# Three y buffers instead of five, and other places for the mixed tiles, in a gated attention and expert block

## The reference

```python
x = x + tanh(g_xattn) * xattn(ctx_512, layernorm(x), Wq, Wk, gamma_raw)     # stage 1
h = layernorm(x)                                                           # 2048 tokens of 512
shared = silu(h @ shared_gate_w) * (h @ shared_up_w) @ shared_down_w
top_val, top_idx = top_k(h @ router_w, 2)
probs = zeros.at[token, top_idx].set(sigmoid(top_val))                      # 2 of 8 are not zero
gate, up = split(einsum('etd,edf->etf', probs.T[:, :, None] * h[None], gate_up_w))
out = x + tanh(g_ffn) * (shared + einsum('eti,eid->etd', silu(gate) * up, down_w).sum(axis=0))
```

## Time and profile before

| | us |
|---|---|
| three runs | 394.82, 396.11, 396.09 |
| median | 396.09 |
| the profiled execution | 394.82 |
| its span, first to last instruction | 393.1 |
| TensorE busy | 360.6 |
| VectorE, ACT, POOL busy | 230.7, 211.9, 144.2 |
| mean granted clock of TensorE | 0.973 |

### The profile page before, as it was taken

One profiled execution on the slowest core, in us unless ns is written; L12 is line 12 of the kernel. 1 busy time (PEld: TensorE's weight loads), 2 busy tenths in 40 slices (PEclk: granted clock), 3 DMA queues, 4 the chain that ended last, 5 costly groups with the idle time before them and its releaser, 6 DMA issues.

```text
span 393.1 us, 6569 instructions
## 1 busy us (share of the span) xinstructions
PE 360.6 (92%) x2024; PEld 202.1 (51%) x2026; DVE 230.7 (59%) x820; ACT 211.9 (54%) x412; POOL 144.2 (37%) x123
## 2 busy tenths in 40 slices
PE   8958789989999999999999999999999989999930
PEld 4513478557845589457875444344344434334610
DVE  1899999899999789960846372451451533601200
ACT  2695888476653686435230576566457466363210
POOL 2200121030533342222214364764745654654331
PEclk9987999999999999999999999999999999999975
DMA  7999980276667633449241845746565656576354
GB/s 218 383 387 380 389 286 6 27 206 174 191 112 170 199 61 40 69 113 207 36 53 29 134 72 95 118 77 111 86 115 87 98 107 115 79 119 109 56 75 53
DMA packets 30649, 53.48 MB, mean 136 GB/s; under 512 B 4758, under 2 KB 8086, under 8 KB 30614
## 3 DMA queue, kind: packets, MB, share of 16 engines
q0 software_dynamic: 11216, 24.52, 38.4%
q1 hardware_dynamic: 19110, 28.40, 20.7%
q10 hardware_dynamic: 288, 0.13, 0.1%
HBM read 28.60 MB, written 24.45 MB: 135 GB/s over the span
## 4 chain that ended last, share of the span: by engine, by line
PE 54%; DMA 20%; DVE 10%; issue 7%; ACT 5%; POOL 2%; POOLq 1%; DVEq 0%; ACTq 0%
PE gate_up L1328 14%; PE down L1374 12%; PE gate_up L1339 11%; DMA out_dram<-x,tmp 8%; DMA out_dram<-tmp,idx 5%; DMA out_dram<-y_sb,idx 4%; DMA out_dram<-y_sb,tmp 4%; PE gate_up L1335 4%; PE turned_x L1308 2%; DVE ge_words L1761 2%; ACT junk L731 1%; PE down L1365 1%; PE front L1204 1%; ACT x L768 1%; DVE top L1802 1%
## 5 line engine op out<-in xcount | busy, mean ns | idle before, releaser
L1339 PE MATMUL gate_up<-w_gu,xT 128*128 x192 | 86.2, 593 | 0.0
L1328 PE MATMUL gate_up<-xT,w_shgu 128*128 128x128 f32 x544 | 63.8, 276 | 1.1 <-ACT xT L779 1.1
L1328 PEld LDWEIGHTS gate_up<-xT,w_shgu 128*128 128x128 f32 x544 | 62.2, 192 | 3.6 <-issue 2.3
L565 POOL DMA_INDIRECT xg<-x_rows,idx x34 | 40.4, 1189 | 43.6 <-DMA x_rows<-payl 13.5
L1339 PEld LDWEIGHTS gate_up<-w_gu,xT 128*128 128x128 f32 x192 | 34.8, 190 | 35.9 <-issue 35.9
L2096 DVE SCALAR_TENSOR_TENSOR h<-gate_up,p_t,silu 128x256 f32<-128x256 f32 x33 | 15.9, 483 | 57.8 <-ACT silu L802 48.5
L1374 PE MATMUL down<-w_dn,hT 128*128 x100 | 47.0, 596 | 0.0
L2067 DVE COPY sim<-w_gu 128x2048 f32 x36 | 42.4, 1229 | 1.4 <-issue 0.7
L591 POOL DMA_INDIRECT out_dram<-y_sb,idx x14 | 24.2, 1728 | 44.5 <-ACT y_sb L835 16.3
L731 ACT ACTIVATE junk<-sim,probe 128x512 int8<-128x512 f32 x44 | 31.2, 712 | 14.2 <-DVE probe L1752 7.3
L835 ACT ACTIVATE y_sb<-down,gates 128x512 f32<-128x512 f32 x35 | 23.9, 687 | 27.1 <-PE down L1374 18.1
(11 more groups left out here) (239 smaller groups left out, 545.1 us busy)
## 6 DMA issues: line engine op xcount, KB each, us to landing
w_gu<-in_L_ffn_gate_up_w_dram SPq DMA_DIRECT2D x8, 1024.0 KB, 12.5
xs<-in_x_dram SPq DMA_DIRECT2D x4, 1024.0 KB, 6.9
w_dn<-in_L_ffn_down_w_dram SPq DMA_DIRECT2D x8, 512.0 KB, 10.8
out_dram<-xs SPq DMA_DIRECT2D x4, 1024.0 KB, 6.8
x_rows<-x SPq DMA_DIRECT2D x4, 1024.0 KB, 5.2
out_dram<-y_sb POOLq DMA_DIRECT2D x16, 256.0 KB, 4.3
w_gu<-in_ctx_dram SPq DMA_DIRECT2D x4, 256.0 KB, 5.2
xg<-x_rows,idx POOLq DMA_INDIRECT x34, 4.2
```

The source lines that it names most:

```text
L565: G.indirect_dma_start(out=xg[:, t % XG, :], out_offset=None, in_=x2_rows[0:2 * N, :] if t < EARLY else x2_rows[:, :], in_offset=bass.Indi ...
L1328: mm = TE.matmul(g_b[j % 2][:, f * P:(f + 1) * P], w_shgu[:, c, f * P:(f + 1) * P], xT[:, x_slot(j), c], start=(c == 0), stop=(c == DC - 1))
L1339: mm = TE.matmul(g_b[j % 2][:, :], xT[:, x_slot(j), c], w_gu[:, bass.ds(experts[n] * (DC * F2) + c * F2, F2)], start=(c == 0), stop=(c == ...
```

## The change

Three things. `MIXED` goes from (9, 12, 14, 17, 19, 22, 24, 27, 29) to (9, 11, 13, 15, 18, 21, 24, 27, 30). The calls of `stage_up`, `stage_down` and `scatter_doubles` move with the tiles; all `stage_up` copies of a mixed tile now stand together, where some stood two and two. And the y buffers from job 26 on are three in turn (0, 1, 2) instead of five.

```diff
-    MIXED = (9, 12, 14, 17, 19, 22, 24, 27, 29)
+    MIXED = (9, 11, 13, 15, 18, 21, 24, 27, 30)
...
-    Y_FROM, Y_TURN = 26, (0, 2, 3, 4, 1)
+    Y_FROM = 26
+    assert Y_FROM % 2 == 0
...
     def y_slot(j):
-        return j % 2 if j < Y_FROM else Y_TURN[(j - Y_FROM) % len(Y_TURN)]
+        return j % 2 if j < Y_FROM else (j - Y_FROM) % 3
...
         def y_at(j):
-            return (y_sb[:, 0], y_sb[:, 1], tmp[:, 0, :], x2[:, 2, :], x2[:, 3, :])[y_slot(j)]
+            return y_sb[:, y_slot(j)] if y_slot(j) < 2 else tmp[:, 0, :]
...
             scatter(12)
+            scatter_doubles(11)
             gather(17)
             scatter(13)
-            scatter_doubles(12)
             gather(18)
             scatter(14)
+            scatter_doubles(13)
...
             scatter(30)
-            scatter_doubles(29)
             scatter(31)
+            scatter_doubles(30)
             scatter(32)
...
-                if y_slot(j) >= 2 and k is None:
+                if y_slot(j) == 2 and k is None:
                     act.wait_ge(scatter_ready, 1)
...
             y_of(27)
             turned_h(28)
+            stage_down(2, 0)
+            stage_down(2, 1)
             silu_of(29)
             turned_rows(14)
             y_of(28)
             turned_h(29)
-            stage_down(2, 0)
-            stage_down(2, 1)
+            stage_down(2, 2)
+            stage_down(2, 3)
...
             stage_up(1, 0)
             stage_up(1, 1)
+            stage_up(1, 2)
+            stage_up(1, 3)
             weight_of(11)
             gate(26)
-            stage_up(1, 2)
-            stage_up(1, 3)
             weight_of(12)
             gate(27)
-            weight_of(13)
-            gate(28)
             stage_up(2, 0)
```

More of the change, by code:

```diff
@@ L676, in _ @@
             scatter(18)
-            scatter_doubles(17)
             gather(23)
             scatter(19)
+            scatter_doubles(18)
             gather(24)
             scatter(20)
-            scatter_doubles(19)
             gather(25)
@@ L686, in _ @@
             scatter(22)
+            scatter_doubles(21)
             gather(27)
             scatter(23)
-            scatter_doubles(22)
             gather(28)
@@ L1053, in _ @@
             turned_h(30)
-            stage_down(2, 2)
-            stage_down(2, 3)
+            stage_down(3, 0)
+            stage_down(3, 1)
             silu_of(31)
@@ L1059, in _ @@
             turned_h(31)
-            stage_down(3, 0)
-            stage_down(3, 1)
+            stage_down(3, 2)
+            stage_down(3, 3)
             silu_of(32)
@@ L1065, in _ @@
             turned_h(32)
-            stage_down(3, 2)
-            stage_down(3, 3)
+            stage_down(4, 0)
+            stage_down(4, 1)
             silu_of(33)
@@ L1071, in _ @@
             turned_h(33)
+            stage_down(4, 2)
+            stage_down(4, 3)
             silu_of(34)
@@ L1075, in _ @@
             turned_h(34)
-            stage_down(4, 0)
-            stage_down(4, 1)
             silu_of(35)
@@ L1081, in _ @@
             turned_h(35)
-            stage_down(4, 2)
-            stage_down(4, 3)
+            stage_down(5, 0)
+            stage_down(5, 1)
             silu_of(36)
@@ L1087, in _ @@
             turned_h(36)
-            stage_down(5, 0)
-            stage_down(5, 1)
+            stage_down(5, 2)
+            stage_down(5, 3)
             silu_of(37)
@@ L1093, in _ @@
             turned_h(37)
-            stage_down(5, 2)
-            stage_down(5, 3)
             silu_of(38)
@@ L1099, in _ @@
             turned_h(38)
+            stage_down(6, 0)
+            stage_down(6, 1)
             silu_of(39)
@@ L1103, in _ @@
             turned_h(39)
-            stage_down(6, 0)
-            stage_down(6, 1)
+            stage_down(6, 2)
+            stage_down(6, 3)
             silu_of(40)
@@ L1109, in _ @@
             turned_h(40)
-            stage_down(6, 2)
-            stage_down(6, 3)
             silu_of(41)
@@ L2311, in _ @@
             stage_up(2, 3)
+            weight_of(13)
+            gate(28)
             weight_of(14)
             gate(29)
+            stage_up(3, 0)
+            stage_up(3, 1)
+            stage_up(3, 2)
+            stage_up(3, 3)
             weight_of(15)
             gate(30)
-            stage_up(3, 0)
-            stage_up(3, 1)
             weight_of(16)
             gate(31)
-            stage_up(3, 2)
-            stage_up(3, 3)
+            stage_up(4, 0)
+            stage_up(4, 1)
+            stage_up(4, 2)
+            stage_up(4, 3)
             weight_of(17)
@@ L2325, in _ @@
             gate(33)
[L2326 to L2329, removed]
             weight_of(19)
             gate(34)
+            stage_up(5, 0)
+            stage_up(5, 1)
+            stage_up(5, 2)
+            stage_up(5, 3)
             weight_of(20)
             gate(35)
-            stage_up(5, 0)
-            stage_up(5, 1)
             weight_of(21)
             gate(36)
-            stage_up(5, 2)
-            stage_up(5, 3)
             weight_of(22)
             gate(37)
-            weight_of(23)
-            gate(38)
             stage_up(6, 0)
@@ L2347, in _ @@
             stage_up(6, 3)
+            weight_of(23)
+            gate(38)
             weight_of(24)
@@ L2353, in _ @@
             stage_up(7, 1)
+            stage_up(7, 2)
+            stage_up(7, 3)
             weight_of(26)
             gate(41)
-            stage_up(7, 2)
-            stage_up(7, 3)
             weight_of(27)
```

2 lines of the change are left out of this document (1 added, 1 removed).

## The result

| | before | after |
|---|---|---|
| median of 6 runs each, us | 395.41 | 399.09 |
| lowest to highest, us | 392.78 to 396.11 | 397.46 to 400.45 |
| the profiled execution, us | 394.82 | 401.78 |
| mean granted clock of TensorE | 0.973 | 0.969 |
| store of tile 11, of tile 32, at us | 250.61, 381.99 | 254.71, 388.69 |

The ratio is 1.0101, with a 95% interval of 1.0058 to 1.0144: slower by 1.0%, and the medians are 3.7 us apart. The forecast was +1.3, inside the half per cent; the change costs more than that, and the time lies in the range. The profiled pair is 7.0 us apart, since the profiled execution after was slower than any of the six behind the median: the profile shows which steps grew, and their sum is larger than what a median has.

A forecast was written before the change was run, and what follows sets the result against it. The prediction took POOL's serial queue of stores to bound the kernel, TensorE close behind. Its terms, -2.4 + 1.4 + 2.6 = +1.6, rounded down to +1.3, on the median 396.09 gave 397.4 us; range 393.2 to 401.5.

The forecast's parts named there:

- signs: Tile 11's y 5 us late, TensorE gap 2 to 4 us, store 32 at 382 to 385, leads shrinking to 2 or 3.
- What bounds the kernel: From about 280 us to the end, POOL's serial queue of stores decides, with TensorE at nearly the same pace.
- (a): Places of mixed tiles: three gaps of two count instead of four, one twin-store wait less, -2.4 us.
- (b): Tile 11's y waits for tile 9's twin store, so its store is issued later: +1.4 us, bounds -0.1 and +2.9.
- TensorE loses 3.4: Work queued on ACT behind tile 11's y delays `turn_h(29)` from 251.78 to 255.2, without reaching the end by itself.
- (c): Later y buffers wait for twin stores: TensorE 0 to 1.5 us each for tiles 13 and 15, stores' path nothing.
- (d): VectorE's weight copies in fours, not pairs, stretch POOL's store issues in four mixed tiles: +2.6 us, bounds 0 and +5.2.
- TensorE as the bound: Rival: TensorE loses 7.9 us, more than its lead, and decides the end; +4 to +5, about 400.5, chance 0.25.
- Faster: Rival: the queue catches up where gaps are three, with steps of 5.55; time about 393, chance 0.16.
- Whole groups keep POOL out: Rival: groups of copies hold POOL's issues for their whole rest, +6.0 for +2.6; +4.7, about 401, chance 0.07.

The follow-up runs named there:

- e2: The changed kernel with five y buffers back, so new places and copies in fours alone; 398.82 against 396.02 for the kernel before, 1.0058.
- e3: The changed kernel with its three y buffers in the turn 0, 2, 1, so tile 11's y goes to `tmp`; 399.30 against 396.02, 1.0079.
- e1: The kernel before, old places, with three y buffers in the turn 0, 1, 2 instead of five; 400.46 against 396.02, 1.0112.
- e4: The kernel before with all VectorE weight copies of a mixed tile four in a row, places and buffers unchanged; 397.87 against 396.02, 1.0037.
- f4: e2 with the weight copies of its last five mixed tiles two and two, a gate between; 398.84 against 396.96 for the kernel before, 1.0047.
- g3: e2 with pairs of copies waiting for POOL's gather of tile j-14, placed at other gates than in g1; 399.06 against 396.37, 1.0048.
- h1: f4 with its last 20 weight copies done by a multiplication by 1.0 that also writes a sum; 392.23 against 396.87 for the kernel before, 0.9883.
- g1: e2 with pairs of copies from the third mixed tile on waiting for POOL's gather of tile j-13; 410.01 against 395.52, 1.0361.

## Why the prediction was right or wrong

- **The number** fell into the range with some luck. The forecast was set on 396.09; the median before is now 395.41, and on the old one the 3.7 would have given 399.8, outside the forecast's own 395 to 399.3. Of its signs, the late y of tile 11 and the gap of TensorE (3.15) came; store 32 came at 388.69 and not at 382 to 385, the clock did fall, and the lead did not shrink to 2 or 3 (4.8 at tile 16, 5.2 at tile 31).
- **What bounds the kernel** was right: the serial queue of stores sets the end. Lengthening VectorE's copies by 20 us shortened the program, because the stores' issues became shorter.
- **(a)** -2.4: met in the profiled pair, with the step to tile 11 counted apart. That step is a wait for a twin store as well, since tile 11 is mixed now: with it there are four in the changed kernel, as in e2, against four before.
- **(b)** y of tile 11: it came at 253.75 and not 251.2, since the stores of tiles 8 and 9 were stretched and tile 9's twin store was issued at 248.50, not at 245.29. In the step it is +0.9 for +1.4, within the bounds, but not for the reason given: the step is 8.1 in e2 and 8.0 in e3 as well, where y of tile 11 doesn't wait. The store of tile 11 waits for tile 9's twin store whatever y does, so the +0.9 comes from the places. On the old places, where it doesn't, the y wait made that step 2.1 longer (e1). e3, without TensorE's wait, gains 0.2%. Taking the buffers away costs 1.7 us (after over e2).
- **TensorE loses 3.4**: too small. `turn_h(29)` came 5.75 later, of which 0.9 was already there at store 7 (227.65, before 226.75), and I had named the fall of the clock only as a possible addition. It did not reach the end by itself, as forecast: the lead of tile 31 is 5.2.
- **(c)** charged the path of the stores nothing. ACT's y in `tmp` waits six times (tiles 18, 21, 24, 27, 30 and 33) for the twin store of the mixed tile three before, 22.8 us, a good deal more than the 1.5 allowed per tile; but TensorE's waits are short (0.7 and 0.4) behind tile 11, so it stays nearly free.
- **(d)** is the step that failed, in size and in reasoning. The mechanism was named: an issue meets the copies and is stretched by 0.3 to 1.6. I counted the tiles whose copies change from pairs to fours, 4 x 1.3 x 1/2 = 2.6. e4 puts exactly that, on the old places, at +1.5. The profiled pair has +7.3 instead, and the medians, with (a) and (b) as above, leave 3.7 + 2.4 less 0.9 to 1.7 for (b), which is 4.4 to 5.2; this is a subtraction, not a measurement. The reason is in the timelines: not the shape of the groups, which f4 shows to be indifferent on the new places, but when the stores come. Stores did not meet the copies of mixed tiles more often: eleven overlap them before, eight after. But before, nine of the eleven took 1.58 to 2.00 (a single copy, or the rest of one, in their way) and only two more; after, all eight took 2.19 to 3.05, and the store behind each mixed tile falls into the copies every third tile. I took "half of the issues are gathers" as a chance, drawn anew each time, and it is a phase that repeats.
- **The other rivals.** TensorE as the bound: it decided in g3, not here, where no lead behind tile 12 is under 1.8. Faster: the plain steps, 6.13, never came near the 5.55 that it needed.
- **Whole groups keep POOL out**, the rule weighed there: no. The longest issues of a store are 3.05 (after), 3.48 (h1) and 3.54 (e3) with up to four copies of 1.2 in a row; nothing near 4.7 was seen. I asked whether an issue is held by one copy or by the group; the rows say by one copy at a time, and up to twice: the 3.17 at 276.42 and the 3.05 at 324.88 are such double holds, and so is the twin store of 3.07 in the earlier trace rows, which the forecast left out when it spoke of one stretched row.
- **Not settled**: why the phase settles where it does. My reading is that the old gaps of two move a store against the copies now and then, and that an equal gap of three, 18.3 us, with the queue running at TensorE's pace, keeps the same encounter for good; e1, which has the old gaps and still 7.3 us of stretch, shows that a change of the leads alone is enough to bring the meeting about. This is argued. The runs that moved the copies (g1 to g3) moved the bound too. Nor was h1's copy tried on the old places or with three buffers.

## What to carry to other kernels

Where a chain of GpSimd-issued DMAs sets the end, look at the duration of each issue, not only at waits: a figure that jumps from 1.58 to 2 to 3 us names another engine's work as a cost. Whether two periodic activities on different engines collide is a matter of phase, so price it by laying the two timelines side by side: a meeting cost between nothing and 1.96 us here (3.54 - 1.58), by where in the issue the copies fell, and it can repeat every time. And the longer instruction can be the cheaper one: VectorE had time to spare, so a copy of twice the length that leaves the shared port alone won 1.6%, where moving copies and waits about won nothing.

## What the runs showed of the hardware

- An indirect accumulating store of 128 x 512 takes 1.58 us to issue when VectorE is quiet or works in the accumulating form, and up to 3.54 (e3) when it meets plain 128 x 2048 copies. Some that meet them are hardly touched: one that begins 0.2 us before them took 1.59 (232.35 in the profile before), but one that begins 0.57 before them took 2.19 (305.82 in f4).
- Of 92 such issues above 1.65 us in the fourteen traces, 91 end 0.06 to 0.12 or 1.40 to 1.48 us after the end of one plain copy.
- A plain copy of 128 x 2048 takes 1.23 us, the form with the sum 2.28.
- TensorE's clock was granted at 0.51 for some 2 us after a wait of 3.15 us between matmuls, once it worked again.
